# Layer norms multiplied out by ScalarE instead of VectorE, turned 128 tokens at a time; GpSimd's sums of the rotation as a piece of their own, biases and one norm at other places in the order

## What is computed

```python
x  = L0_attn_hidden_states                       # (2, 1024, 256)
xn = layernorm(x)                                # (x - mean) / sqrt(var + 1e-5), no weights
x  = x + linear_attention(xn) + ternary_ffn(xn)  # layer 0: elu+1 features, 16 heads of 16;
                                                 #   silu(up) * gate, weights cut to -s, 0, s
xn = layernorm(x)
x  = x + softmax_attention(xn) + hadamard_ffn(xn)  # layer 1: rotary positions on q and k,
                                                   #   silu(gate) * up between two Hadamard turns
```

## Time and profile before

| | |
|---|---|
| three runs | 783.95, 780.44, 783.94 us; median 783.94 us |
| the profiled execution | 779.61 us, span 777.8 us from the first to the last instruction |
| busy in the span | PE 712.5 us (92%), DVE 550.7 (71%), ACT 435.9 (56%), POOL 288.7 (37%) |
| mean granted TensorE clock | 0.969 |

### The profile page before, as it was taken

The page is one execution under the profiler, slowest core; times in us unless marked ns, Lnnn a source line. Parts: engine busy times, 40 slices in busy tenths (PEclk is TensorE's granted clock), DMA queues, the critical chain, the costliest instruction groups (busy, mean ns, idle before and its releaser), DMA issues.

```text
span 777.8 us, 10975 instructions
## 1 busy us (share of the span) xinstructions
PE 712.5 (92%) x4190; PEld 446.3 (57%) x4190; DVE 550.7 (71%) x896; ACT 435.9 (56%) x579; POOL 288.7 (37%) x273
## 2 busy tenths in 40 slices
PE   3778898969697979999999999999999999999997
PEld 3657787957456868867767676333333433333444
DVE  4897766675557674667888878888888378888416
ACT  2542223345244444243243333999999899999883
POOL 0156865332314566343344343012224213422510
PEclk9898999998799989999999999999999999999999
DMA  6145101000301345334311002344344345342221
GB/s 247 55 155 186 52 0 55 1 1 1 108 0 40 125 155 196 103 106 146 110 55 55 24 32 72 108 131 132 113 138 140 90 133 172 126 131 84 95 85 55
DMA packets 25704, 74.14 MB, mean 95 GB/s; under 512 B 4604, under 2 KB 5980, under 8 KB 24692
## 3 DMA queue, kind: packets, MB, share of 16 engines
q1 hardware_dynamic: 21124, 65.37, 25.1%
q0 software_dynamic: 3808, 7.60, 3.3%
q10 hardware_dynamic: 720, 0.48, 0.2%
HBM read 54.54 MB, written 23.06 MB: 100 GB/s over the span
## 4 chain that ended last, share of the span: by engine, by line
PE 73%; DVE 13%; ACT 5%; issue 4%; POOL 3%; DMA 1%; SPq 0%; DVEq 0%; ACTq 0%; POOLq 0%
PE PS L734 23%; PE PS L996 16%; PE PS L982 11%; PE PS L740 10%; PE PS L965 6%; PE PS L955 4%; DMA stg<-in_wa 1%; DVE mx L1275 1%; DVE XD L1081 1%; PE PS L814 1%; DVE sg L1213 1%; DVE sg L1204 1%; DVE XL L1088 1%; ACT sg L1415 1%; DVE bst L1066 1%
## 5 line engine op out<-in xcount | busy, mean ns | idle before, releaser
L1461 ACT ACTIVATE P<-PS 128x1024 f32<-128x1024 f32 x256 | 249.0, 1024 | 29.9 <-PE PS L982 29.7
L1282 DVE TENSOR_REDUCE mx<-PS 128x1 f32<-128x512 f32 x300 | 189.1, 682 | 32.1 <-PE PS L965 30.5
L1275 DVE TENSOR_REDUCE mx<-PS 128x2 f32<-128x1024 f32 x106 | 124.8, 1220 | 37.9 <-PE PS L955 37.6
L996 PE MATMUL PS<-P,VV 128*32 128x512 f32 x1024 | 136.5, 605 | 0.1
L1538 POOL TENSOR_TENSOR hl<-sg,hh 128x512 fp32r<-128x512 f32 x64 | 83.1, 1299 | 137.1 <-ACT hh L1423 79.9
L982 PEld LDWEIGHTS PS<-QS,KS 64*128 64x128 f32 x512 | 48.4, 183 | 123.2 <-ACT P L1461 110.2
L982 PE MATMUL PS<-QS,KS 64*128 64x512 f32 x512 | 116.6, 456 | 2.3 <-DVE mx L1275 1.8
L965 PE MATMUL PS<-KM,QM 64*128 64x512 f32 x300 | 81.3, 396 | 0.0
L1417 ACT ACTIVATE sg<-PS,cols 128x512 f32<-128x512 f32 x32 | 22.0, 688 | 83.0 <-PE PS L734 83.0
L734 PE MATMUL PS<-XH,UGH 128*128 128x512 f32 x128 | 54.9, 429 | 5.8 <-ACT us L1426 4.9
L1547 POOL TENSOR_TENSOR sg<-sg,us 128x512 f32<-128x512 f32 x32 | 42.1, 1315 | 37.2 <-ACT us L1426 37.2
(11 more groups left out here) (201 smaller groups left out, 1417.5 us busy)
## 6 DMA issues: line engine op xcount, KB each, us to landing
QM<-scr_q SPq DMA_DIRECT2D x16, 512.0 KB, 4.3
KM<-scr_k SPq DMA_DIRECT2D x16, 512.0 KB, 5.3
QS<-scr_q SPq DMA_DIRECT2D x16, 512.0 KB, 4.3
KS<-scr_k SPq DMA_DIRECT2D x16, 512.0 KB, 5.3
scr_q<-spl SPq DMA_DIRECT2D x24, 256.0 KB, 3.3
scr_k<-spl SPq DMA_DIRECT2D x24, 256.0 KB, 3.6
scr_o<-OE POOLq DMA_DIRECT2D x14, 256.0 KB, 2.7
stg<-in_tern SPq DMA_DIRECT2D x3, 1024.0 KB, 4.8
```

Source lines behind the costliest of these rows:

```text
L996: i = e.matmul(PS[32 * c:32 * c + 32, 7, :], v_head(8 * b + kt, 2 * j + c // 2), P[s % 4][:, chunk(c // 2 + 2 * (c % 2))], start=(kt == 0) ...
L1275: e.tensor_reduce(mx[p % 2][:, :, qt, half], PS[:, b:b + 2, :], AX.X, ALU.max).then_inc(q["mx"], 2)
L1282: e.tensor_reduce(mx[p % 2][:, h, qt, half:half + 1], bank[b], AX.X, ALU.max).then_inc(q["mx"], 1)
L1461: e.activation(P[s % 4][:, half * 1024:(half + 1) * 1024], PS[:, b:b + 2, :].rearrange("p b n -> p (b n)"), ACT.Exp).then_inc(q["ex"], 1)
```

## The change

1. `ln_norm` moves from VectorE to ScalarE. VectorE still inverts rstd and now also makes nmr = -mean * rstd (one instruction of 128 x 4); ScalarE computes Identity(rstd * x + nmr), four instructions of 128 x 256 with both factors as columns, each of which counts up `lnn`.
2. `ln_turn` on TensorE waits for each 128 tokens apart and turns their two blocks into the two banks in turn. The first bank is therefore complete with the seventh block, not the fourth.
3. The first turn waits for the identity matrix alone (semaphore `idn`), not for all four constants. The first norm stands ahead of the second's statistics.
4. The four `bias` pieces of layer 0 and the load of the second bias (`load_ob1`) stand later; VBB is made earlier, in the new `spread_vb`.
5. GpSimd's sums of the rotation leave `qk` and become `qk_join`, some steps later.
6. The norm of chunk 2 of layer 1 begins at step 2 of chunk 3 in place of step 8.

```diff
+cols idn c ob wsd x0 ...            (a semaphore of its own for the identity)
     def qk(c, n, count):
         put("qk", c, n, ps.next(), ps.next())
         yield
-        for _ in range(count):
+        for k in range(count):
             yield
+            if k == 0:
+                put("qk_join", c, n)
         put("qk_split", c, n)
     def side0():
         bf = 0
         for n, _ in enumerate(attention0()):
+            if n in (13, 15, 17, 19):
+                put("bias", 0, (n - 13) // 2)
+            if n == 20:
+                put("load_ob1")
...
                     put("scales")
+                    put("spread_vb")
                     put("load_wa1")
...
-    NORMS = {(0, 2, 2): 0, (0, 2, 13): 1, (0, 3, 8): 2, (1, 0, 5): 3}
+    NORMS = {(0, 2, 2): 0, (0, 2, 13): 1, (0, 3, 2): 2, (1, 0, 5): 3}
...
-    for i in (0, 1, 0):
+    for i in (0, 0, 1):
         next(ln0[i])
     put("w0h")
...
-        if n > 7:
-            put("bias", 0, n - 8)
     put("half")
     put("load_down")
-    put("load_ob1")
...
+        if split and k == split_at - 5:
+            put("qk_join", *split)
         if split and k >= split_at:
             put("qk_split", *split)
# TensorE, ln_turn
-                e.wait_ge(q["lnn"], n + 1)
                 if n == 0:
-                    e.wait_ge(d["c"], 64)
-                for k, b in enumerate(banks):
-                    for t in range(4):
+                    e.wait_ge(d["idn"], 16)
+                for t in range(4):
+                    e.wait_ge(q["lnn"], 4 * n + t + 1)
+                    for k, b in enumerate(banks):
                         i = e.transpose(bank[b][:, t * 128:(t + 1) * 128], ln_buffer(n)[:, t, k * 128:(k + 1) * 128], IDN[:, :])
-                    i.then_inc(q["lnb"], 1)
-                    freed[b] = q["lnl"], 2 * n + k + 1
+                        if t == 3:
+                            i.then_inc(q["lnb"], 1)
+                            freed[b] = q["lnl"], 2 * n + k + 1
# VectorE, ln_norm
-                for t in range(4):
-                    o = e.tensor_scalar(ln_buffer(n)[:, t, :], X[:, 4 * c + t, :], mv[i][:, t, 0:1], rstd[i][:, t:t + 1], ALU.subtract, ALU.mult)
-                o.then_inc(q["lnn"], 1)
+                e.wait_ge(q["lnr"], 2 * n + 1)
+                e.scalar_tensor_tensor(nmr[i][:, :], mv[i][:, :, 0], -1.0, rstd[i][:, :], ALU.mult, ALU.mult).then_inc(q["lnr"], 1)
# ScalarE, new
+            def ln_norm(n):
+                c, i = n % 4, n % 2
+                e.wait_ge(q["lnr"], 2 * n + 2)
+                if n == 7:
+                    e.wait_ge(q["lnb"], 14)
+                for t in range(4):
+                    e.activation(ln_buffer(n)[:, t, :], X[:, 4 * c + t, :], ACT.Identity, bias=nmr[i][:, t:t + 1], scale=rstd[i][:, t:t + 1]).then_inc(q["lnn"], 1)
# GpSimd
-            def qk(c, n, *banks):
+            def qk_join(c, n):
```

More of the change, by code:

```diff
@@ L42 @@
 DMAS = """
-cols c ob wsd x0 x1 x2 x3 st0 st1 cs pad sp0 sp1 sp2 sp3 km0 km1 qm0 qm1 ks0 ks1 qs0 qs1 m0 m1
+cols idn c ob wsd x0 x1 x2 x3 st0 st1 cs pad sp0 sp1 sp2 sp3 km0 km1 qm0 qm1 ks0 ks1 qs0 qs1 m0 m1
 oe0 oe1 num0 num1 rc0 rc1 rs0 rs1 late0 late1 late2 late3 wl y
@@ L483, in program @@
         mv = [sb(f"mv{i}", 207.5 + i / 32, [128, 4, 2]) for i in range(2)]
+        nmr = [sb(f"nmr{i}", 207.625 + i / 32, [128, 4]) for i in range(2)]
         rstd = [sb(f"rstd{i}", 207.5625 + i / 32, [128, 4]) for i in range(2)]
@@ L1063, in ln_stats @@
                     e.wait_ge(q["lnv"], n - 1)
-                    e.wait_ge(q["lnn"], n - 1)
+                    e.wait_ge(q["lnr"], 2 * (n - 1))
                 for t in range(4):
@@ L1099, in signs @@
                 e.wait_ge(d["cols"], 16)
-                e.wait_ge(d["c"], 64)
+                e.wait_ge(d["c"], 48)
                 a, z = COLS["suu"][0], COLS["sud"][0]
@@ L1123, in tern_cut, with spread_vb, add_vb @@
                 e.scalar_tensor_tensor(t, stg[i][:, js], hi, r32(t), ALU.is_gt, ALU.subtract).then_inc(q["tt"], 1)
-            def add_vb(b):
+            def spread_vb():
                 for k in range(2):
                     e.tensor_scalar(VBB[:, k, :], ONES[:, :], col("vb1", k), None, ALU.mult).then_inc(q["vbb"], 1)
+            def add_vb(b):
                 e.wait_ge(d["ob"], 32)
@@ L1331, in last @@
                         e.tensor_tensor(xs, bank[banks[2 + 2 * cc + i]], xs, ALU.add).then_inc(q["ly"], 1)
-            parts = {f.__name__: f for f in (start, ln_stats, ln_norm, ln_turn, bias, w0l, signs, tern_scale, tern_cut, add_vb, half, scales, kv_in, kv_sums, q0,
+            parts = {f.__name__: f for f in (start, ln_stats, ln_norm, ln_turn, bias, w0l, signs, tern_scale, tern_cut, spread_vb, add_vb, half, scales, kv_in, kv_sums, q0,
                                              kv_sum, att_n, att_t, att_b, gate, up, ffn_end, prep_down, prep_ug, qk, qk_split, max_half, max_join, recip, join, project, last)}
@@ L1343, in start @@
                 e.dma_start(cols[:, :], cols_d).then_inc(d["cols"], 16)
-                for t, src in ((IDN, ident_d), (MASK, mask_d), (HAD, had_d), (BKV, bkv_d)):
+                e.dma_start(IDN[:, :], ident_d).then_inc(d["idn"], 16)
+                for t, src in ((MASK, mask_d), (HAD, had_d), (BKV, bkv_d)):
                     e.dma_start(t[:, :], src).then_inc(d["c"], 16)
@@ L1352, in ln_stats @@
                 if n >= 2:
-                    e.wait_ge(q["lnn"], n - 1)
+                    e.wait_ge(q["lnn"], 4 * (n - 1))
                 e.activation(rstd[i][:, :], mv[i][:, :, 1], ACT.Sqrt, bias=col("eps5")).then_inc(q["lnd"], 1)
+            def ln_norm(n):
[5 more added lines that the diff above has]
+                    e.activation(ln_buffer(n)[:, t, :], X[:, 4 * c + t, :], ACT.Identity, bias=nmr[i][:, t:t + 1], scale=rstd[i][:, t:t + 1]).then_inc(q["lnn"], 1)
             def ln_turn(n, *banks):
@@ L1483, in last @@
                     e.activation(LH[:, qs], OE[0][:, qs], ACT.Copy).then_inc(q["lh"], 1)
-            parts = {f.__name__: f for f in (start, ln_stats, ln_turn, w0h, tern_abs, kv_in, q0, att_t, prep_attn1, prep_down, prep_ug, gate, up,
+            parts = {f.__name__: f for f in (start, ln_stats, ln_norm, ln_turn, w0h, tern_abs, kv_in, q0, att_t, prep_attn1, prep_down, prep_ug, gate, up,
                                              hidden, qk_split, v, max_rows, scores, out, load_exp, last)}
@@ L1494, in bias @@
                 xs = X[:, 4 * c:4 * c + 4, :]
-                e.wait_ge(q["lnn"], 4 * layer + c + 1)
+                e.wait_ge(q["lnn"], 4 * (4 * layer + c + 1))
                 if layer == 0:
@@ L1608, in low @@
                     e.wait_ge(q["fill"], 2)
-            parts = {f.__name__: f for f in (bias, fold, kv_in, q0, butterfly, prep_attn1, up, hidden, ones_v, qk, load_wl, out, recip, times, high, low)}
+            parts = {f.__name__: f for f in (bias, fold, kv_in, q0, butterfly, prep_attn1, up, hidden, ones_v, qk_join, load_wl, out, recip, times, high, low)}
             for name, *args in order:
```

5 lines of the change are left out of this document (1 added, 4 removed).

## The result

The changed kernel takes 785.6 us (median of 16 runs, 782.93 to 787.56), the kernel before 781.28 us in its 16 (779.1 to 783.95): ratio 1.0052, 95% interval 1.0037 to 1.0067, so 4.1 us or 0.5% slower, where 2.7 us faster was forecast. (The forecast of 781.2 us started from a median of three runs, 783.9; from that of sixteen, 781.3, it would have been 778.6.) The profiled execution took 785.97 us, with a span of 784.2.

The account below looks back on a forecast made before the run. TensorE, busy 92%, was taken to bound the kernel, with gaps almost all before 282 us. Terms A to G summed to -2.7 us, from 783.9 to 781.2 us; the range leaving out 2 in 10 runs was 774 to 789.

Parts of the forecast that it names:

- A: The start: third norm on ScalarE makes XH 2.1 us later, VectorE gets 1.1 back, new block order costs 0.3; +1.3 us.
- E: Norms of chunks 0 and 1 of layer 1, now on ScalarE ahead of a tanh, plus late first banks; +1.7 us.
- B: 57 to 80 us: moved biases beside VectorE hold kvb, the cuts and scales, and VBB adds 0.5; +3.1 us.
- C: Fourth bias ahead of first butterfly and minimum at 87.56: 2.4 us later, less 1.6 slack at AL; +0.8 us.
- D: VBB made early: TensorE's wait of 1.52 us at 107.03 goes; -1.5 us.
- F: Norm of chunk 2 of layer 1 moved earlier: 6.7 us won, 3.8 and 0.6 lost; -2.3 us.
- G: Rotation's sums later: the 4.16 us wait at 281.40 and 2.5 us of slow clock go, 0.9 returns; -5.8 us.
- the sums' move does nothing: Rival: a later piece holds the product sg x us as well; 787 us, counted inside "no change", no chance of its own.
- ScalarE's queue becomes the path: Rival: everything behind norms 1 to 5 is awaited, costing 11.9 us; 790 us, within slower outcomes given 0.20 together.

Follow-up runs that it names:

- vnorm: Changed kernel with all eight norms multiplied out on VectorE again, turns as changed; ratio 1.0031 against the kernel before (+2.4 us).
- fourth_only: Changed kernel with the first three biases of layer 0 back at their old places, the fourth and load_ob1 at the new; ratio 1.0013 against the kernel before.
- bias_back: Changed kernel with all four biases of layer 0 and load_ob1 back at their old places; ratio 0.9959 against the kernel before (-3.2 us).
- norm_spread: Kernel before with only the earlier norm of chunk 2 of layer 1 and the early VBB (spread_vb); ratio 0.9928, -5.6 us.
- norm2: Kernel before with only the norm of chunk 2 of layer 1 started six steps earlier; ratio 0.9966, -2.7 us.
- sums: Kernel before with only the rotation's sums made a later piece of their own (qk_join); ratio 0.9995, -0.4 us.
- combo_v: Kernel before with later sums, earlier chunk 2 norm, early VBB, and VV's blocks reversed so the first eight lie clear of the transfer; ratio 0.9913, -6.8 us.
- one_scalar: Like combo_v (VV's blocks reversed), but chunk 3's norm of layer 1 on ScalarE, start and turns as changed; ratio 0.9910 against the kernel before, -7.0 us.
- combo_late: Kernel before with later sums, earlier chunk 2 norm, early VBB, and VV's ones and first product of v three steps later; ratio 0.9907, -7.3 us.
- bias: Kernel before with only the four biases of layer 0 and load_ob1 at their new places; ratio 1.0076, +5.9 us.

## Why the prediction was wrong

| term | predicted | measured | from |
|---|---|---|---|
| A + E, ScalarE's norms and the new turns | +3.0 | +1.6 | changed less vnorm (without the new turns, which both have) |
| B, three biases, VBB | +3.1 | +3.0 | changed less fourth_only (without VBB, which both have) |
| C, the fourth bias | +0.8 | +4.2 | fourth_only less bias_back |
| D, early VBB | -1.5 | -3.0 | norm_spread less norm2 |
| F, earlier norm | -2.3 | -2.7 | norm2 |
| G, later sums | -5.8 | -0.4 | sums; 0.0 beside F and D |

They add up to +2.7, and each difference of two runs is uncertain by 1 to 2 us; the change cost 4.1, and no run says where the other 1.4 lie.

**G failed, and it is the larger miss (5.4 us).** The step "with the product first, that 4.16 us wait goes, and so do the 2.5 us lost in five us at half clock" held: lateness falls from 6.5 to 0.1 us between 282 and 286 us. What failed is that I stopped there, with "I subtract 0.9 for a new short wait", on the ground that "after that it waits for next to nothing". That was true of a TensorE that came there late by the wait and the low clock. The work on the other side, hh, the halves, their transfer, the ones and VV, had the same finishing time as before, or a later one, as it now stood behind the sums. The kernel before had the signs of it: a wait of 0.15 us for VV at 296.73, and at the third product of v, 299.62, a copy that had ended 0.27 us earlier (298.99 + 0.36). I had listed the rival "the sums' move does nothing" with another cause (a later piece that holds the product), and gave it no chance of its own. Its sum, 3.1 us slower, is the one that came nearest to the 4.1 measured.

**C failed (3.4 us).** "AL ended at 90.77 and TensorE used it at 92.35: 1.58 us of slack." TensorE needs not only what AL writes, but also the bank that AL reads, and kvb,QP at 90.83 took that bank: the slack was 0.06 us, and 2.3 of the bias's 2.4 us reached TensorE. The rest is the lower clock behind the longer wait and at 137 us, for which C had no term, less 1.2 us won at the old place.

**B came out at its size by luck.** It took half of what the cut and `scales` could lose. All three instructions that could be held were held, kvb and `scales` by a bias, the cut by the hl behind one: 2.18 us for 1.10, 2.20 for 1.33 and 2.33 for 0.15, 4.1 us in all where I had 1.0 + 0.5 + 1.1. And all of it reached TensorE, here in fourth_only and in the changed kernel:

```profile
82.06 0.76 PE L824 MATMUL PS<-kvb,QP 128*128 128x136 f32 x4 [2.92 <-DVE at L1192]
```

```profile
86.51 1.28 PE L822 MATMUL PS<-kvb,QP 128*128 128x136 f32 x4 [5.13 <-DVE at L1190]
```

At this product the changed kernel is 4.4 us later, and at the next, behind AL, too (99.36 against 94.93). 1.5 us came back by 104 us, since from 95 to 99 us fourth_only ran at 0.66 of the clock and the changed kernel at 1.00. By the Trainium skill's rule on the shared interfaces (GPSIMD Engine Reference, 8. Key points), taken as GpSimd always first, B would by the prediction be at its upper bound of 5.1 us (its parts give 1.0 + 1.0 + 2.2 + 0.5 = 4.7). The rows agree with the rule for the cut and `scales`, which read two tensors in SBUF, though GpSimd was not always first; kvb reads one, and no row shows in what mode.

**A** was right in its row: XH of chunk 2 at 29.17 us, 1.9 later than in the earlier trace rows, and four products of the norm in 2.06 to 2.08 us against 2.1 forecast. nmr took 0.17 us alone, but 0.76 and 0.92 beside GpSimd (202.30, 282.99), where I had 0.3 with its semaphore. The start was 1.4 us late at 41 us, which leaves little of the 1.6 for **E**, forecast at 1.7: with the new turns it cost 0.4, TensorE being 6.8 us late at 165 us and 7.2 at 222.92. **D** and **F** held in place, and F, within the uncertainty, in size: TensorE does not wait at VBB's product (113.88); F's new waits came at 238 to 243 us (UGL, 0.70 and 1.67 us). D gave 2.0 us at that product, and norm_spread's trace gains another 1.4 on norm2's by 144 us, where norm2's clock fell at 134 us and norm_spread's did not. The rival "ScalarE's queue becomes the path", at 11.9 us for the norms, did not come: they cost 1.6.

**The version to keep** is norm_spread: two edits, 5.6 us or 0.7% faster than before. combo_v, one_scalar and combo_late lie at 6.8, 7.0 and 7.3 us, not told from it by their intervals. What stays open is which of the small waits in the chain behind hh could be taken without a new one. Later ones, VV in reverse and chunk 3's norm on ScalarE (one_scalar) gave nothing that the intervals tell from zero, and the sums of chunks 2 and 3 back behind their products made it slower. No run shortened the work of GpSimd itself in this stretch, so that it is what limits the gain is read from the traces and not tested.

## What to carry to other kernels

Before a removed wait is booked as a gain, look for the next products that depend on the engines that were waited for, and at their wait or slack now: a wait near zero (0.15 us here) or a slack near zero (0.27) means that those engines finish just in time, and the gain ends there. The slack of an instruction ends with the first use of what it writes or of the buffer that it frees, whichever comes first. A term that comes out at its size is not thereby right: B's parts were half of what happened, and a higher clock elsewhere gave back the difference. Elementwise work moved on GpSimd is priced by what it lands beside on VectorE, and a lengthened wait of TensorE also by the clock behind it.

## What the runs showed of the hardware

VectorE's instructions were held until an instruction of GpSimd ended that had begun first, in the changed kernel and in the run bias: one of 128x1 took 2.33 us in place of 0.15 and one of 128x8 2.18 in place of 1.10 beside a bias of 128x1024, one of 128x1024 2.20 in place of 1.33 beside an hl. It went the other way as well: a bias takes 2.34 to 2.40 us, and took 3.37 and 3.29 where a cut of VectorE had begun 0.2 us before it. ScalarE's four 128x256 products with two column factors took 2.08 us beside GpSimd as well (283.94, with the sums running; 2.06 to 2.08 in all eight norms), where VectorE's four took 4.92 us in the same place (run sums). The clock fell to its lower level at 490 us too, where the changed kernel had no long wait ahead that the kernel before lacked. All nineteen other kernels traced have such a fall of 3 to 7 us between 478 and 501 us, and only the trace of the kernel before has none. That trace is of one of its faster executions (779.61 us, of 779.1 to 783.95), so a difference of 2 us at that place between two traces says nothing of the change.
